# Four groups of TensorE matmuls in another order in each double step of a fused attention and convolution kernel

## The chip, the cores and the metric

The kernel runs on one core of a Trainium2 chip. The metric is the device time of one execution in microseconds (us), lower is better. The kernel before takes 6069.41 us, the median of three runs (6067.23 to 6069.91).

## The reference

The input x is 8 images of 192 channels, 128 by 128 pixels, all float32. Two layers follow one another. Layer 0 normalises x in 32 groups, projects every pixel to query, key and value (192 channels each, six heads of 32), and cuts each image into windows of 8 by 8 pixels, so 256 windows an image and 64 tokens a window. Per window and head:

```
o    = irfft2(rfft2(q * SCALE) * rfft2(k))          # 8 by 8 circular convolution, per channel
attn = softmax(o @ v^T + bias)                      # 64 x 64, bias depends on head and position
y    = attn @ v
x1   = x + proj(y) + proj_b
```

Layer 1 normalises x1 in 32 groups again, adds to every pixel its Laplacian (4 times itself less its four neighbours), multiplies by the 192 x 192 matrix merge_w, and adds merge_b and x1.

## The kernel before, in words

Everything is done in one long loop, software-pipelined by hand. The unit is a pair of windows side by side: 64 tokens each, so 128 tokens fill the partitions. There are 1024 pairs. A double step j handles two pairs and five stages of different age at once; `pair(lag)` in the code gives the double step that is in the stage of that lag, and is empty at the two ends of the loop. There are 512 double steps with attention work (j = 0 to 511), and then 76 in which only layer 1 is left.

In the double step j TensorE does in this order:

- `qkv(2j)`: query, key and value of the first new pair, ten matmuls into PSUM tile `b_q` (line 481).
- `m_slot(2j)`: a piece of layer 1's merge product, into `b_s` (lines 432 to 443), or nothing.
- half of the projection of lag 4 (lines 486 and 489).
- `qkv(2j+1)`, behind the semaphore `lo_out`: VectorE's remainder of the first pair (`qkl`, line 874) reads the same part of `b_q`.
- transposes of the values (line 518) and of lag 3's softmax P (line 528), the other half of the projection, `m_slot(2j+1)`.
- the group y = P times V of lag 3 (line 546), which waits for ScalarE's copy `probsT`; 48 matmuls in the trace.
- the inverse transform of lag 1 (line 556) from `prod` into `b_q`, 24 matmuls in the trace; it waits for `lo_out`.
- the forward transform of lag 0 (line 570) from `qkh` and `qkl` into the four banks of `b_t`, twelve matmuls; its second half waits for `yT_out`, since y lies in two of these banks.
- the scores of lag 1 (line 587) from `osb`, ScalarE's copy of the inverse transform, and `vT`, into `b_s`, 48 matmuls in the trace.

The scores write nearly all of `b_s`, which the merge pieces and the projection also use. So their first matmul waits for four semaphores: `o_out` (ScalarE has copied the inverse transform), `s_out`, `x1_done` (VectorE has taken the projection out, line 913) and `m_read` (VectorE has taken the merge piece of `m_slot(2j+1)` out, line 758).

VectorE goes through its own fixed list in each double step: the scores of lag 2 in its count, which are those that TensorE has just made, plus the bias (line 880), the maximum of them (L885), `qkl` of the first pair, the product of the two transforms (L891), statistics, the merge result (L758), one part of the stencil of layer 1 (lines 719, 727 and 735), `qkl` of the second pair, the sum of the softmax (L905), the projection's result (L913), the reciprocal (L923), in odd double steps the remainder `xhl` (L927), the merge result of `m_slot(2j+1)` (L758), and then border and statistics (L744, L621). GpSimd does two passes over the softmax (L1036 after the maximum, L1047 after the reciprocal) and in odd double steps the remainder `xl` (L1042), behind L1036. ScalarE copies out of PSUM (helper line 940) and does the exponential (L1004).

What a double step holds depends on j modulo 4; four double steps are one block of eight rows of pixels. In the texts below they are called a, b, c and d for j mod 4 = 0, 1, 2, 3. From block 18 on (of 0 to 127 with attention) the stencil runs, from block 19 on the merge pieces: two in each of a, b and c, none in d. The stencil's L735 stands in b, c and d; L927 and L1042 stand in b and d; the border L744 stands in d. In blocks in which the next image's statistics are gathered (the first 12 of 16 in an image) L621 stands at the end of each double step.

Of the kernel before, what the change touches and what calls it, by code (L numbers as in the profile page):

```python
# [16 lines left out]
N = WS * WS  # L17
QK, QKV = 2 * C, 3 * C
G, CG, GP = 32, 6, 4
EPS = 1e-5  # L20
NF = 94
# [72 lines left out]
def program(nc, x, out, w):  # L94
# [15 lines left out]
    with ExitStack() as ctx:  # L110
# [17 lines left out]
        fwd, fwdh, fwdl = sb("fwd_sb", [128, NF]), sb("fwdh", [128, NF], F32R), sb("fwdl", [128, NF], F32R)  # L128
        inv = sb("inv_sb", [NF, N])
# [227 lines left out]
        def _(pe):  # L357
            mm = nc.tensor.matmul
# [134 lines left out]
            for j, pair in doubles():  # L493
# [39 lines left out]
                if pair(4):  # L533
                    project(b_r[:, 256:512], 3).then_inc(proj_mm, 1)
                m_slot(2 * j + 1, pair)
                if pair(3):
                    k, n = pair(3)
                    pe.wait_ge(pT_out, n)
                    if pair(0):
                        pe.wait_ge(vT_out, pair(0)[1])  # L540
                    for i in range(2):
                        for h in range(NH):
                            for win in range(2):
                                rows = slice(win * N, (win + 1) * N)
                                q, c = (h * HD, i * N) if h < 4 else (i * N + (h - 4) * HD, 2 * N)
                                last = mm(q_banks[q:q + HD, 2 + win, c:c + N],  # L546
                                          vs[rows, (2 * k + i) % 8, h * HD:(h + 1) * HD],
                                          probsT[rows, i, h, :], start=True, stop=True)
                    last.then_inc(y_mm, 1)
                if pair(1):  # L550
                    pe.wait_ge(prod_done, pair(1)[1])
                    if pair(0):
                        pe.wait_ge(lo_out, 2 * j + 2)
                    for k in range(6):
                        for g in range(2):
                            last = mm(o_out_ps[g * N:(g + 1) * N, k * N:(k + 1) * N],  # L556
                                      prod[:, g * 6 + k, :, :].rearrange("p h d -> p (h d)"), inv[:, :],
                                      start=True, stop=True)
                    last.then_inc(o_mm, 1)
                if pair(0):  # L560
                    pe.wait_ge(lo_out, 2 * j + 2)
                    for i in range(2):
                        if i == 1 and pair(3):
                            pe.wait_ge(yT_out, pair(3)[1])
                        elif i == 1:
                            pe.wait_ge(vT_out, pair(0)[1])
                        for k, (ff, xx) in enumerate(((fwdh, qkh), (fwdh, qkl), (fwdl, qkh))):
                            for win in range(2):
                                rows = slice(win * N, (win + 1) * N)
                                last = mm(q_banks[0:NF, 2 * i + win, 0:QK], ff[rows, :], xx[rows, i, :],  # L570
                                          start=(k == 0), stop=(k == 2))
                    last.then_inc(t_mm, 1)
                if pair(1):
                    i, n = pair(1)
                    pe.wait_ge(o_out, n)
                    if pair(2):
                        pe.wait_ge(s_out, pair(2)[1])
                    if pair(4):
                        pe.wait_ge(x1_done, pair(4)[1])
                    pe.wait_ge(m_read, d_count[2 * j + 1])  # L580
                    for k in range(6):
                        for g in range(2):
                            for h in range(2):
                                s = g * 6 + k
                                t, q = divmod(s, 4)
                                r = (g * 2 + h) * HD
                                last = mm(scores[h * N:(h + 1) * N, s * N:(s + 1) * N], osb[r:r + HD, k, :],  # L587
                                          vT[r:r + HD, i % 2, q // 2, t - g, q % 2 * N:q % 2 * N + N],
                                          start=True, stop=True)
                    last.then_inc(s_mm, 1)  # L590

        @block.vector
        def _(dve):
# [341 lines left out]
        def _(act):  # L935
# [3 lines left out]
            def copy(o, i):  # L939
                return A.activation(o, i, ACT.Copy)  # L940
# [44 lines left out]
            for j, pair in doubles():  # L985
                blk, ph = divmod(2 * j, 8)
                img, c = divmod(blk, NS)
                if ph == 0 and c == 13 and 0 <= img < B - 1:
                    sqrt(cst[:, 3, :], cst[:, 2, :])
                if ph == 0 and c == 2 and 1 <= img <= B:  # L990
                    sqrt(sm[:, 6, :], sm[:, 4, :])
                h = (j + 2) // 2
                a_result(2 * j)
                if pair(0):
                    v_copy(2 * j)
                    high(2 * j)
                split(h, 0 if j % 2 == 0 else 2)
                if pair(0):
                    v_copy(2 * j + 1)
                if pair(2):  # L1000
                    i, n = pair(2)
                    act.wait_ge(sub_done, n)
                    pr = probs[:, i % 2, :, :].rearrange("p s m -> p (s m)")
                    A.activation(pr, pr, ACT.Exp).then_inc(exp_done, 1)  # L1004
                if pair(0):
                    high(2 * j + 1)
                    act.wait_ge(vT_mm, pair(0)[1])
                    copy(vT[:, j % 2, :, :, :].rearrange("p i t n -> p (i t n)"), q_banks[:, 2, :]).then_inc(vT_out, 1)
                if pair(3):
                    act.wait_ge(pT_mm, pair(3)[1])  # L1010
                    copy(probsT[:, :, :, :].rearrange("p i h n -> p i (h n)"), q_banks[:, 0:2, 0:6 * N]
                         ).then_inc(pT_out, 1)
                a_result(2 * j + 1)
                if j % 2 == 0:
                    split(h, 1)
                if pair(3):
                    act.wait_ge(y_mm, pair(3)[1])
                    copy(yT[:, :, :, :].rearrange("p i w n -> p w i n"),
                         q_banks[:, 2:4, 0:3 * N].rearrange("p w (i n) -> p w i n", n=N)).then_inc(yT_out, 1)
                if pair(1):  # L1020
                    act.wait_ge(o_mm, pair(1)[1])
                    copy(osb[:, :, :].rearrange("p k n -> p (k n)"), o_out_ps).then_inc(o_out, 1)
                if pair(0):
                    act.wait_ge(t_mm, pair(0)[1])
                    copy(qh[:, :, :], q_banks[0:NF, :, 0:C]).then_inc(qh_out, 1)
# [54 lines left out]
```

## Time and profile before

| quantity | value |
|---|---|
| median of 3 runs | 6069.41 us |
| the profiled execution | 6063.48 us |
| its span, first to last instruction | 6061.7 us |
| TensorE matmul busy | 5826.5 us, 96% |
| VectorE busy | 5059.8 us, 83% |
| ScalarE busy | 3165.5 us, 52% |
| GpSimd busy | 2011.1 us, 33% |
| granted TensorE clock, mean | 0.997 |

The profile is of one execution. Instruction starts are in us from the span's start. Matmuls overlap one another in the records, so the time of a group of matmuls is best read from its first start to the first start of the next group. TensorE's time between its groups is small; VectorE is the second busiest engine.

### The profile page before, as it was taken

The numbers are of one execution on the slowest core, as the hardware profiler recorded it, in microseconds if no ns is written. First come the engines' busy times: TensorE is split into PE (matmuls) and PEld (weight loads), VectorE is DVE, ScalarE is ACT, GpSimd is POOL, SyncE is SP. The second block draws the span as 40 slices with busy tenths as digits, with TensorE's granted clock in tenths as the row PEclk, the third lists the DMA queues.
The fourth block names the chain that finished last, engine by engine and source line by source line (L and its number), as shares of the span: only waits on it lengthen the run. The fifth ranks groups of instructions, "written<-read, shape, count | busy, mean of one in ns | idle before, by whom it ended". The sixth has DMA issues, their size and how long they took to land.

```text
span 6061.7 us, 210224 instructions
## 1 busy us (share of the span) xinstructions
PE 5826.5 (96%) x93708; PEld 5135.1 (85%) x93708; DVE 5059.8 (83%) x8287; ACT 3165.5 (52%) x6020; POOL 2011.1 (33%) x1286
## 2 busy tenths in 40 slices
PE   7999999999999999999999999999999999999987
PEld 5888888888888888888888888888888888888876
DVE  4777788888888888888888888888888888888876
ACT  2555555555555555555555555555555555555531
POOL 1333333333333333333333333333333333333310
PEclk9999999999999999999999999999999999999999
DMA  4221123323333233332333323332333322222235
GB/s 130 71 58 58 54 75 104 98 81 93 95 104 101 75 92 99 101 97 80 95 101 100 93 80 93 106 101 86 86 96 98 106 84 69 82 79 75 80 93 163
DMA packets 392599, 550.79 MB, mean 91 GB/s; under 512 B 24918, under 2 KB 284825, under 8 KB 391706
## 3 DMA queue, kind: packets, MB, share of 16 engines
q1 hardware_dynamic: 391708, 537.35, 30.9%
q8 instruction: 750, 12.29, 0.8%
q14 instruction: 141, 1.16, 0.1%
HBM read 335.93 MB, written 201.33 MB: 89 GB/s over the span
## 4 chain that ended last, share of the span: by engine, by line
PE 82%; DVE 8%; ACT 7%; issue 1%; DMA 1%; SPq 0%; DVEq 0%
PE b_q L481 22%; PE b_t L570 10%; PE b_s L587 7%; PE b_q L556 7%; PE b_t L546 6%; PE b_s L489 5%; PE b_s L486 5%; PE b_t L528 4%; PE b_s L432 3%; PE b_s L434 3%; PE b_t L518 3%; ACT qkh L940 2%; DVE qkl L874 2%; PE b_s L441 2%; PE b_s L443 2%; PE b_s L442 2%
## 5 line engine op out<-in xcount | busy, mean ns | idle before, releaser
L1047 POOL TENSOR_TENSOR probs<-probs,srec 128x768 f32<-128x768 f32 x512 | 880.7, 1720 | 2211.8 <-DVE srec L923 2211.8
L1036 POOL TENSOR_TENSOR probs<-probs,smax 128x768 f32<-128x768 f32 x512 | 754.1, 1473 | 1519.7 <-DVE smax L885 1519.7
L880 DVE TENSOR_TENSOR probs<-b_s,posb 128x768 f32<-128x768 f32 x512 | 488.3, 954 | 660.3 <-PE b_s L587 659.4
L940 ACT ACTIVATE vs<-b_q 128x192 f32<-128x192 f32 x1024 | 339.2, 331 | 1294.3 <-PE b_q L481 1294.3
L481 PE MATMUL b_q<-wnh,xh 128*128 128x288 f32 x2048 | 700.7, 342 | 67.0 <-DVE qkl L874 65.7
L874 DVE TENSOR_TENSOR qkl<-b_q,qkh 128x384 fp32r<-128x384 f32 x1024 | 566.5, 553 | 176.9 <-ACT qkh L940 139.7
L489 PEld LDWEIGHTS b_s<-yT,wp 128*128 128x128 f32 x4096 | 618.5, 191 | 52.3
L489 PE MATMUL b_s<-yT,wp 128*128 128x128 f32 x4096 | 622.4, 275 | 0.0
L486 PE MATMUL b_s<-yT,wp 128*128 128x256 f32 x2048 | 613.5, 381 | 1.5 <-DVE probs L880 0.9
L481 PE MATMUL b_q<-wnl,xhl 128*128 128x288 f32 x2048 | 606.5, 296 | 0.0
L481 PE MATMUL b_q<-wnh,xhb 128*128 128x288 f32 x2048 | 606.3, 296 | 0.0
L940 ACT ACTIVATE qh<-b_t 94x768 f32<-94x768 f32 x512 | 412.7, 806 | 369.7 <-PE b_t L570 369.7
L481 PE MATMUL b_q<-wnh,xl 128*128 128x288 f32 x2048 | 604.1, 295 | 0.0
L481 PE MATMUL b_q<-wnl,xh 128*128 128x288 f32 x2048 | 603.0, 294 | 0.0
L940 ACT ACTIVATE qkh<-b_q 128x384 fp32r<-128x384 f32 x1024 | 497.6, 486 | 166.4 <-PE b_q L481 166.4
L940 ACT ACTIVATE yT<-b_t 128x384 f32<-128x384 f32 x512 | 251.0, 490 | 629.3 <-PE b_t L546 629.3
L587 PEld LDWEIGHTS b_s<-vT,osb 32*64 32x64 f32 x24576 | 409.0, 133 | 174.7 <-issue 173.8
L587 PE MATMUL b_s<-vT,osb 32*64 32x64 f32 x24576 | 477.3, 221 | 27.1 <-DVE late L758 16.6
L885 DVE TENSOR_REDUCE smax<-probs 128x12 f32<-128x768 f32 x512 | 488.0, 953 | 17.7
L481 PEld LDWEIGHTS b_q<-wnh,xh 128*128 128x128 f32 x2048 | 387.2, 189 | 129.2 <-issue 94.7
L905 DVE TENSOR_REDUCE ssum<-probs 128x12 f32<-128x768 f32 x512 | 481.8, 941 | 0.0
L891 DVE TENSOR_TENSOR prod<-qh,b_t 94x768 f32<-94x768 f32 x512 | 481.2, 940 | 0.0
(155 smaller groups left out, 13688.6 us busy)
## 6 DMA issues: line engine op xcount, KB each, us to landing
ld<-in_x SPq DMA_DIRECT2D x192, 512.0 KB, 4.6
late<-x_dram SPq DMA_DIRECT2D x112, 640.0 KB, 4.8
xs<-in_x SPq DMA_DIRECT2D x128, 512.0 KB, 5.4
x_dram<-late SPq DMA_DIRECT2D x128, 512.0 KB, 3.0
out<-late SPq DMA_DIRECT2D x128, 512.0 KB, 3.0
late<-x_dram SPq DMA_DIRECT2D x240, 192.0 KB, 5.4
xs<-in_x SPq DMA_DIRECT2D x128, 256.0 KB, 5.9
x_dram<-late SPq DMA_DIRECT2D x128, 256.0 KB, 3.7
```

Of the source, the lines that this page charges most:

```text
L481: last = mm(o, xx[:, h % 2, at], ww[:, par, t, lo:up], start=(k == 0), stop=(k == 4))
L486: mm(o, wp[:, k, :], both, start=True, stop=False)
L489: last = mm(o.rearrange("p (r i w c) -> p i r w c", r=WS, i=2, w=2)[:, i], wp[:, k + 1 + i, :], rest, start=False, stop=(i == 1))
L570: last = mm(q_banks[0:NF, 2 * i + win, 0:QK], ff[rows, :], xx[rows, i, :], start=(k == 0), stop=(k == 2))
L587: last = mm(scores[h * N:(h + 1) * N, s * N:(s + 1) * N], osb[r:r + HD, k, :], vT[r:r + HD, i % 2, q // 2, t - g, q % 2 * N:q % 2 * N + N] ...
L874: V.tensor_tensor(qkl[:, i % 2, :], q_out, qkh[:, i % 2, :].bitcast(F32), ALU.subtract).then_inc(lo_out, 1)
L880: V.tensor_tensor(scored(i).rearrange("p (t q) m -> p t q m", q=4), scores.rearrange("p (t q m) -> p t q m", q=4, m=N), posb[:, :, :].unsq ...
L885: V.tensor_reduce(smax[:, i % 2, :], scored(i), AX.X, ALU.max).then_inc(max_done, 1)
L905: V.tensor_reduce(ssum[:, i % 2, :], scored(i), AX.X, ALU.add).then_inc(sum_done, 1)
L940: return A.activation(o, i, ACT.Copy)
L1036: P.tensor_tensor(probs[:, i % 2, :, :], probs[:, i % 2, :, :], smax[:, i % 2, :].unsqueeze(2).broadcast_to([128, 12, N]), ALU.subtract).t ...
L1047: P.tensor_tensor(probs[:, i % 2, :, :], probs[:, i % 2, :, :], srec[:, i % 2, :].unsqueeze(2).broadcast_to([128, 12, N]), ALU.mult).then_ ...
```

## The change

Line numbers in the diff's new part are those of the changed kernel. The double step's four last groups on TensorE stood in the order P times V, inverse transform, forward transform, scores. They now stand in the order inverse transform, P times V, scores, forward transform. Each keeps its own waits. On ScalarE the copy of the inverse transform (`osb`) now stands ahead of the copy of y (`yT`). VectorE's, GpSimd's and the DMA queue's lists are not touched, and no instruction is added or removed.

```
@@ TensorE, double step j, behind m_slot(2 * j + 1, pair) @@
+                if pair(1):
+                    pe.wait_ge(prod_done, pair(1)[1])
+                    if pair(0):
+                        pe.wait_ge(lo_out, 2 * j + 2)
+                    for k in range(6):
+                        for g in range(2):
+                            last = mm(o_out_ps[g * N:(g + 1) * N, k * N:(k + 1) * N],
+                                      prod[:, g * 6 + k, :, :].rearrange("p h d -> p (h d)"), inv[:, :],
+                                      start=True, stop=True)
+                    last.then_inc(o_mm, 1)
                 if pair(3):
                     k, n = pair(3)
                     pe.wait_ge(pT_out, n)
...
                     last.then_inc(y_mm, 1)
-                if pair(1):
-                    pe.wait_ge(prod_done, pair(1)[1])
...
-                    last.then_inc(o_mm, 1)
-                if pair(0):
-                    pe.wait_ge(lo_out, 2 * j + 2)
-                    for i in range(2):
-                        if i == 1 and pair(3):
-                            pe.wait_ge(yT_out, pair(3)[1])
-                        elif i == 1:
-                            pe.wait_ge(vT_out, pair(0)[1])
...
-                    last.then_inc(t_mm, 1)
                 if pair(1):
                     i, n = pair(1)
                     pe.wait_ge(o_out, n)
                     if pair(2):
                         pe.wait_ge(s_out, pair(2)[1])
                     if pair(4):
                         pe.wait_ge(x1_done, pair(4)[1])
                     pe.wait_ge(m_read, d_count[2 * j + 1])
...
                     last.then_inc(s_mm, 1)
+                if pair(0):
+                    pe.wait_ge(lo_out, 2 * j + 2)
+                    for i in range(2):
+                        if i == 1 and pair(3):
+                            pe.wait_ge(yT_out, pair(3)[1])
+                        elif i == 1:
+                            pe.wait_ge(vT_out, pair(0)[1])
+                        for k, (ff, xx) in enumerate(((fwdh, qkh), (fwdh, qkl), (fwdl, qkh))):
+                            for win in range(2):
+                                rows = slice(win * N, (win + 1) * N)
+                                last = mm(q_banks[0:NF, 2 * i + win, 0:QK], ff[rows, :], xx[rows, i, :],
+                                          start=(k == 0), stop=(k == 2))
+                    last.then_inc(t_mm, 1)
@@ ScalarE, double step j, last three copies @@
+                if pair(1):
+                    act.wait_ge(o_mm, pair(1)[1])
+                    copy(osb[:, :, :].rearrange("p k n -> p (k n)"), o_out_ps).then_inc(o_out, 1)
                 if pair(3):
                     act.wait_ge(y_mm, pair(3)[1])
                     copy(yT[:, :, :, :].rearrange("p i w n -> p w i n"),
                          q_banks[:, 2:4, 0:3 * N].rearrange("p w (i n) -> p w i n", n=N)).then_inc(yT_out, 1)
-                if pair(1):
-                    act.wait_ge(o_mm, pair(1)[1])
-                    copy(osb[:, :, :].rearrange("p k n -> p (k n)"), o_out_ps).then_inc(o_out, 1)
```

On TensorE, from the second m_slot of a steady double step to the next double step's qkv, the program before has these rows, with what each first matmul waits for (L546 is P times V, L556 the inverse transform, L570 the forward transform, L587 the scores):

```order
L434 MATMUL b_s<-late,mn 128x256
L546 MATMUL b_t<-probsT,vs 32x64 [waits vT_out,pT_out]
L546 MATMUL b_t<-probsT,vs 32x64 x23
L556 MATMUL b_q<-inv_sb,prod 64x64 [waits lo_out,prod_done]
L556 MATMUL b_q<-inv_sb,prod 64x64 x11
L570 MATMUL b_t<-qkh,fwdh 94x384 [waits lo_out]
L570 MATMUL b_t<-qkh,fwdh 94x384 [waits yT_out]
L587 MATMUL b_s<-vT,osb 64x64 [waits x1_done,m_read,s_out,o_out]
L587 MATMUL b_s<-vT,osb 64x64 x23
L481 MATMUL b_q<-wnh,xh 128x288 [waits xhl_done,xl_done,xh_done]
```

The changed program has these there, at the same place (its L542 is the inverse transform, L556 P times V, L574 the scores, L588 the forward transform):

```order
L434 MATMUL b_s<-late,mn 128x256
L542 MATMUL b_q<-inv_sb,prod 64x64 [waits lo_out,prod_done]
L542 MATMUL b_q<-inv_sb,prod 64x64 x11
L556 MATMUL b_t<-probsT,vs 32x64 [waits vT_out,pT_out]
L556 MATMUL b_t<-probsT,vs 32x64 x23
L574 MATMUL b_s<-vT,osb 64x64 [waits x1_done,m_read,s_out,o_out]
L574 MATMUL b_s<-vT,osb 64x64 x23
L588 MATMUL b_t<-qkh,fwdh 94x384 [waits lo_out]
L588 MATMUL b_t<-qkh,fwdh 94x384 [waits yT_out]
L481 MATMUL b_q<-wnh,xh 128x288 [waits xhl_done,xl_done,xh_done]
```

The scores, with their four semaphores, moved from behind the forward transform to ahead of it; the inverse transform is now the first of the four.

On ScalarE, the copies at the end of a double step and the first of the next, before:

```order
L940 ACTIVATE probsT<-b_t 128x768 [waits pT_mm]
L940 ACTIVATE yT<-b_t 128x2x3x64 [waits y_mm]
L940 ACTIVATE osb<-b_q 128x384 [waits o_mm]
L940 ACTIVATE qh<-b_t 94x768 [waits t_mm]
L940 ACTIVATE vs<-b_q 128x192 [waits v_mm]
```

and in the changed program:

```order
L940 ACTIVATE probsT<-b_t 128x768 [waits pT_mm]
L940 ACTIVATE osb<-b_q 128x384 [waits o_mm]
L940 ACTIVATE yT<-b_t 128x2x3x64 [waits y_mm]
L940 ACTIVATE qh<-b_t 94x768 [waits t_mm]
L940 ACTIVATE vs<-b_q 128x192 [waits v_mm]
```

The copies yT and osb have changed places; qh, the copy of the forward transform, still follows them.

## Rows read from the trace of the kernel before

**Rows 1.** Page, part 4: the chain that ended last, by engine.

```profile
PE 82%; DVE 8%; ACT 7%; issue 1%; DMA 1%; SPq 0%; DVEq 0%
```

**Rows 2.** Waits of TensorE: total us, times, longest us.

```profile
PE b_q L481 <- DVE qkl L874: 65.7, 164, 1.3
PE b_s L587 <- DVE late L758: 16.6, 12, 1.5
PE b_s L432 <- issue: 15.9, 60, 1.1
```

**Rows 3.** Timeline, TensorE, a step b: start us, us, instruction [idle before <-releaser].

```profile
3433.16 0.40 PE L481 MATMUL b_q<-wnh,xh 128*128 128x288 f32 x1
...
3440.63 0.77 PE L546 MATMUL b_t<-probsT,vs 64*32 64x64 f32 x48
...
3442.18 0.41 PE L570 MATMUL b_t<-qkh,fwdh 64*94 64x384 f32 x2
...
3443.56 0.93 PE L587 MATMUL b_s<-vT,osb 32*64 32x64 f32 x48
```

**Rows 4.** Timeline, VectorE, the same step b.

```profile
3435.31 0.56 DVE L874 TENSOR_TENSOR qkl<-b_q,qkh 128x384 fp32r<-128x384 f32 x1
...
3437.64 0.96 DVE L735 SCALAR_TENSOR_TENSOR late<-late 128x512 f32<-128x512 f32 x1
...
3442.93 0.48 DVE L758 SCALAR_TENSOR_TENSOR late<-b_s,mc,late 128x256 f32<-128x256 f32 x1
...
3444.54 0.96 DVE L880 TENSOR_TENSOR probs<-b_s,posb 128x768 f32<-128x768 f32 x1 [0.53 <-PE b_s L587]
```

**Rows 5.** Timeline, ScalarE, the start of the same step b.

```profile
3434.13 0.33 ACT L940 ACTIVATE vs<-b_q 128x192 f32<-128x192 f32 x1 [0.90 <-PE b_q L481]
3434.79 0.49 ACT L940 ACTIVATE qkh<-b_q 128x384 fp32r<-128x384 f32 x1 [0.33 <-PE b_q L481]
```

**Rows 6.** Timeline, GpSimd, xl in the step b and in the next step d.

```profile
3436.76 1.29 POOL L1042 TENSOR_TENSOR xl<-xs,xh 128x512 fp32r<-128x512 f32 x1
...
3459.96 1.74 POOL L1042 TENSOR_TENSOR xl<-xs,xh 128x512 fp32r<-128x512 f32 x1
```

**Rows 7.** Timeline, VectorE, L735 in the step c between.

```profile
3448.89 0.68 DVE L735 SCALAR_TENSOR_TENSOR late<-late 128x512 f32<-128x512 f32 x1
```

**Rows 8.** Timeline, VectorE, ScalarE and TensorE, that step d.

```profile
3460.46 1.78 DVE L735 SCALAR_TENSOR_TENSOR late<-late 128x512 f32<-128x512 f32 x1
...
3461.12 0.48 ACT L940 ACTIVATE qkh<-b_q 128x384 fp32r<-128x384 f32 x1
...
3461.97 0.82 ACT L940 ACTIVATE probsT<-b_t 128x768 f32<-128x768 f32 x1
...
3462.17 0.54 DVE L874 TENSOR_TENSOR qkl<-b_q,qkh 128x384 fp32r<-128x384 f32 x1
3462.19 0.61 PE L489 MATMUL b_s<-yT,wp 128*128 128x128 f32 x4
...
3462.84 0.77 PE L546 MATMUL b_t<-probsT,vs 64*32 64x64 f32 x48
...
3465.60 0.93 PE L587 MATMUL b_s<-vT,osb 32*64 32x64 f32 x48
```

**Rows 9.** Timeline, TensorE, the start of the step a behind it; and a step b.

```profile
3466.46 0.40 PE L481 MATMUL b_q<-wnh,xh 128*128 128x288 f32 x1
...
3469.99 0.38 PE L481 MATMUL b_q<-wnh,xh 128*128 128x288 f32 x1
...
3436.25 0.38 PE L481 MATMUL b_q<-wnh,xh 128*128 128x288 f32 x1
```

**Rows 10.** Timeline, the one double step without forward transform, j = 512.

```profile
5833.68 0.92 PE L556 MATMUL b_q<-inv_sb,prod 94*64 94x64 f32 x24
...
5834.65 0.49 ACT L940 ACTIVATE osb<-b_q 128x384 f32<-128x384 f32 x1 [0.37 <-PE b_q L556]
5835.19 0.93 PE L587 MATMUL b_s<-vT,osb 32*64 32x64 f32 x48 [0.59 <-ACT osb L940]
```

More of the change, by code:

```diff
@@ L549, in _ @@
                     last.then_inc(y_mm, 1)
-                if pair(1):
-                    pe.wait_ge(prod_done, pair(1)[1])
-                    if pair(0):
-                        pe.wait_ge(lo_out, 2 * j + 2)
[L554 to L558, printed above, removed]
-                    last.then_inc(o_mm, 1)
-                if pair(0):
-                    pe.wait_ge(lo_out, 2 * j + 2)
-                    for i in range(2):
-                        if i == 1 and pair(3):
-                            pe.wait_ge(yT_out, pair(3)[1])
-                        elif i == 1:
-                            pe.wait_ge(vT_out, pair(0)[1])
[L567 to L571, printed above, removed]
-                    last.then_inc(t_mm, 1)
                 if pair(1):
```

## The prediction

> **What bounds the kernel now.** I read the chain of waits first. It lies on TensorE for 82% of the span, with 8% on VectorE and 7% on ScalarE [rows 1]. So the order of matmuls costs nothing by itself: the same groups run one after another, and the time changes only where a wait appears or goes. The list of TensorE's waits gives the named ones: 65.7 us in front of `qkv(2j+1)` for `qkl`, 16.6 us in front of the scores for VectorE's merge result, and 60 waits of 15.9 us in front of a merge piece [rows 2]. Then I read the timelines of all engines through one block of four double steps, because the pattern repeats block by block, and asked for each group that moves: what releases it, and how long before it starts.
>
> **Lengths of the groups.** A group's last matmul is modelled to end 0.07 us behind the first start of the next group where nothing waits: the scores of step d end at 3465.60 + 0.93 = 3466.53, and `qkv` starts at 3466.46 [rows 8, 9]. First start to first start, P times V and inverse transform together take 3442.18 - 3440.63 = 1.55 us in step b [rows 3], of which 0.77 - 0.07 = 0.70 is P times V and 0.85 the inverse transform. The scores take 3466.46 - 3465.60 = 0.86. In step d, P times V, inverse and forward transform take 3465.60 - 3462.84 = 2.76 together [rows 8], so the forward transform takes 2.76 - 1.55 = 1.21. In step b 1.38 passes between its start and the scores', so a wait lies in that.
>
> **Part 1, the scores come 1.21 us earlier behind their semaphores.** This is the costly part. In step b VectorE has the longest list: it ends the merge result at 3442.93 + 0.48 = 3443.41, and the scores start at 3443.56, 0.15 later [rows 3, 4]. In the old order the forward transform fills the time: without any wait the scores would start at 3442.18 + 1.21 = 3443.39, so 0.17 us is lost. In the new order the two groups ahead of the scores end at 3440.63 + 0.85 + 0.70 = 3442.18; the scores stand until 3443.56, which is 1.38 us, and the forward transform comes afterwards in full. Behind the waiting matmul is all of TensorE, and VectorE's L880 waits for it too. The loss is 1.38 - 0.17 = 1.21 us, if VectorE ends at the same time.
>
> Can VectorE be earlier? It receives the scores 1.21 us earlier, counted from the next `qkv`, so L880 and L885 move up. But L874 stands behind ScalarE's copy: qkh ends at 3434.79 + 0.49 = 3435.28 and L874 starts at 3435.31, with no idle time noted in front of it [rows 4, 5]. That copy hangs on `qkv(2j)`, which is not moved. So VectorE's list behind L874 keeps its place. One instruction in it gets shorter: L735 takes 0.68 in step c [rows 7], 0.96 in step b [rows 4] and 1.78 in step d [rows 8]. In b and d its end is 0.5 us behind the end of GpSimd's L1042: 3438.05 and 3438.60, 3461.70 and 3462.24 [rows 4, 6, 8]. L1042 follows the pass after the maximum, so it moves up by up to 1.21 us: it would end at 3436.84 in b and, with 1.29 us, at 3460.04 in d, ahead of L735's starts at 3437.64 and 3460.46. L735 is then 0.68 in both. In b that takes 0.28 us off the loss: 1.21 - 0.28 = 0.93. The piece in b stands in blocks 19 to 127, 109 of them: **+101 us** (without the relief 109 x 1.21 = 132; with VectorE also earlier through L874, 0).
>
> The Trainium skill, "SBUF — State Buffer", section "SBUF: two separate sides", says that VectorE instructions with two SBUF inputs and GpSimd instructions lock a shared port pair against one another, so that the loser blocks for the whole instruction. The trace agrees: L735 reads two SBUF tensors and ends only behind L1042. By the lock the sum is the one with the relief, and if these were only slow instructions it would be 31 us more.
>
> **Part 2, waits that go.** In step d there is no merge piece. P times V starts at 3462.84, when probsT (3461.97 + 0.82 = 3462.79) is there; the projection ahead of it ends at 3462.19 + 0.61 = 3462.80, so 3462.73 would have been possible and 0.11 us is lost [rows 8]. The inverse transform now stands there and waits instead for L874, which ends at 3462.71; at 0.15 behind that it would start at 3462.86, no gain [rows 8]. But with L735 1.10 us shorter, L874 is bounded only by qkh, 3461.60, and comes 0.56 earlier. Then nothing waits: 109 x 0.11 = **-12 us**; and in the first 18 blocks, whose 72 double steps have the probsT wait and no stencil, 72 x 0.11 = **-8 us**. Between -20 and 0.
>
> **Part 3, step a.** `qkv(2j+1)` starts 3469.99 - 3466.46 = 3.53 us behind `qkv(2j)` in the step a shown, and 3436.25 - 3433.16 = 3.09 in a step b with the same list [rows 3, 9]. The 0.44 us is the merge piece waiting for L880, which VectorE begins late because step d's list was long. It occurs in the 60 waits of [rows 2]. With step d's list 0.56 us shorter it goes: up to 60 x 0.44 = 26 us. I take **-19**, as the chain from L735 through the border to L880 has to stay free; bounds -26 and 0.
>
> **Part 4, the irregular double steps** (image changes, where VectorE's chains of small instructions run): VectorE ends last there, with waits of up to 1.5 us in front of the scores already now, 12 of them [rows 2]. Each loses the cover of 1.21 us: 12 x 1.21 = 15, and some more that were just covered. I take **+20**, bounds 0 and 40.
>
> **Part 5, edits at nothing.** ScalarE's osb is now covered by P times V alone. The double step j = 512 has no forward transform and shows the shortest way: inverse transform from 5833.68, osb, scores at 5835.19, which is 1.51 us [rows 10]; the new order has 0.85 + 0.70 = 1.55. It is hidden by 0.04 us; if the wait took VectorE's 0.15 us behind osb, 1.61 would come out, 0.06 x some 400 = 24 us. The copy qh moves 0.85 us towards v_copy, in front of which ScalarE idles 0.90 [rows 5]: hidden by 0.05; without that cover each 0.1 us costs 50 us over 512 steps. yT has the whole score group before the forward transform's second half needs it. No DMA moves.
>
> **Sum.** 101 - 12 - 8 - 19 + 20 = +82. On the profiled execution 6063.5 + 82 = 6145.5; the median of the runs is 5.9 above it, so 6069.4 + 82 = 6151 us.
>
> **Rivals.**
> - *VectorE follows the scores.* If L885's end, and not qkh, sets L874, VectorE's list moves up with the scores. Then step b loses nothing and the 65.7 us of waits for `qkl` go too: 6069 - 66 - 19 - 20 = 5964. For it: no idle time is noted in front of L874, so L885 ends close to it. Against it: L874 starts 0.03 us behind qkh's end [rows 4, 5], and the qkh copy depends on `qkv(2j)`, which no longer follows the scores. It decides if L874 can start well ahead of 2.1 us behind `qkv(2j)`. Chance 0.07.
> - *No relief from GpSimd.* L735 stays long: 132 in part 1, 0 in part 3, part 2 only the -8, 20 in part 4: +144, 6213. For it: the relief in d rests on L1042 being 0.4 us clear. Chance 0.12.
> - *A narrow cover fails in every step* (osb or qh, part 5): +24 to +50 on top, around 6190. For it: covers of 0.04 and 0.05. Chance 0.15.
> - *Gains and losses meet*: only half of part 1 comes, as VectorE finds slack elsewhere, with parts 2 and 3 in full, and no part 4: +50 - 46 = 6073. Chance 0.05.
> - The forecast itself: 0.61.
>
> The sum's own bounds are 101 to 132, -20 to 0, -26 to 0, 0 to 40. 6098 to 6205 holds the forecast, the third rival and part of the second. What a measurement can tell from no change is about 0.2%, 12 us: faster 0.08, within 0.03, slower 0.89.
>
> **What the profile of the changed kernel would show.** Idle time in front of the scores released by VectorE's L758, about 1.1 us, once in four double steps, some 110 us in all; L735 at 0.68 in every block; step d's L874 behind qkh at once; the 60 waits in front of a merge piece gone; osb and qh waiting as long as now for TensorE, and no wait of the scores for osb. L880 in step b starting before `qkv` does. I am wrong if L758 of step b ends 1.2 us earlier counted from `qkv(2j)`, or if the scores wait for osb in all steps.

## The result and the profile after

Measured: **6236.56 us** (median of 4 runs, 6235.06 to 6238.25) against 6068.32 (4 runs of the kernel before on the same chip, 6065.76 to 6069.91). The ratio is 1.0277 with a 95% interval from 1.0265 to 1.0289: 168 us slower, twice the +82 that was forecast, and outside the stated range of 6098 to 6205.

In the new code the groups have the lines L542 (inverse transform), L556 (P times V), L574 (scores) and L588 (forward transform); VectorE's and ScalarE's lines kept their numbers. The page of the changed kernel, its parts 1 and 4, and one row of part 3:

```profile
span 6236.5 us, 210224 instructions
PE 5854.7 (94%) x93708; PEld 5165.7 (83%) x93708; DVE 4918.0 (79%) x8287; ACT 3168.8 (51%) x6020; POOL 1952.9 (31%) x1286
q8 instruction: 750, 12.29, 0.8%
PE 71%; DVE 21%; ACT 4%; issue 2%; DMA 0%; SPq 0%; DVEq 0%
```

TensorE's share of the chain fell from 82% [rows 1] to 71%, and VectorE's rose from 8% to 21%: an engine that had been busy all through now waits. TensorE's waits (total us, times, longest us) name four places that answer to [rows 2]:

```profile
PE b_s L574 <- DVE late L758: 146.7, 140, 2.0
PE b_q L481 <- DVE qkl L874: 73.4, 176, 1.3
PE b_s L574 <- issue: 40.0, 51, 1.7
PE b_s L432 <- issue: 1.7, 4, 0.4
```

The first row is the predicted wait; before it had 16.6 us in 12 places. The last is the merge piece, 15.9 us in 60 places before. The third was in no step of the prediction. It releases nothing: "issue" is time in which TensorE waited for nothing that the profile shows.

A step b of the changed kernel, all engines. The columns are start us, duration us, instruction, and the idle time before it with its releaser; the rows answer to [rows 3 to 6]:

```profile
3537.27 0.49 ACT L940 ACTIVATE qkh<-b_q 128x384 fp32r<-128x384 f32 x1 [0.33 <-PE b_q L481]
3537.79 0.56 DVE L874 TENSOR_TENSOR qkl<-b_q,qkh 128x384 fp32r<-128x384 f32 x1 [1.30 <-ACT qkh L940]
3538.01 1.27 POOL L1042 TENSOR_TENSOR xl<-xs,xh 128x512 fp32r<-128x512 f32 x1
...
3540.12 0.68 DVE L735 SCALAR_TENSOR_TENSOR late<-late 128x512 f32<-128x512 f32 x1
...
3543.11 0.92 PE L542 MATMUL b_q<-inv_sb,prod 94*64 94x64 f32 x24
...
3543.95 0.77 PE L556 MATMUL b_t<-probsT,vs 64*32 64x64 f32 x48
...
3545.13 0.48 DVE L758 SCALAR_TENSOR_TENSOR late<-b_s,mc,late 128x256 f32<-128x256 f32 x1
...
3545.76 0.93 PE L574 MATMUL b_s<-vT,osb 32*64 32x64 f32 x48 [1.03 <-DVE late L758]
3546.61 0.41 PE L588 MATMUL b_t<-qkh,fwdh 64*94 64x384 f32 x2
3546.74 0.96 DVE L880 TENSOR_TENSOR probs<-b_s,posb 128x768 f32<-128x768 f32 x1 [0.53 <-PE b_s L574]
```

This is the step as the prediction had it. VectorE now stands idle for 1.30 us in front of L874, which still starts 0.03 us behind qkh's end. L758 ends at 3545.61 and the scores start 0.15 us later. From the start of P times V to the scores it is 1.81 us where 0.70 would do: 1.11 lost, less the 0.17 of before, 0.94. GpSimd's xl ends at 3539.28, ahead of L735, which takes 0.68 us.

**Where the 175 us between the two profiled executions are.** I cut both traces at the first `qkv` of each of the first 512 double steps, which gives 511 stretches, and subtracted step from step. They hold 176 us; ahead of them and behind them the changed kernel is 1.3 us shorter. A step has a "gap" when two matmuls that follow one another inside one group start more than 0.6 us apart. "Regular" are steps without gap and half clock whose difference is under 0.5 us or, in a step b with a merge piece (blocks 19 to 127), between 0.8 and 1.05 us.

| steps | number | after minus before, us |
|---|---|---|
| regular b, blocks 19 to 127 | 92 | +85.8 |
| regular a, c, d | 100, 115, 98 | -16.0, +0.2, -2.1 |
| regular b, blocks before 19 | 13 | -0.8 |
| steps with a gap inside the scores or the forward transform | 47 | +49.7 |
| steps that a half-clock stretch touches | 26 | +42.1 |
| other irregular steps | 20 | +17.1 |
| sum | 511 | +176.0 |

So the predicted waits came as computed, and the steps with gaps and with half clock cost about half of the total. Of the steps that half clock touches 12 are steps b; about 11 of their 42 us are the ordinary 0.93 of such a step.

**The gaps.** TensorE alone, in a step where nothing was awaited:

```profile
4046.47 0.77 PE L556 MATMUL b_t<-probsT,vs 64*32 64x64 f32 x48
4047.17 0.69 PE L574 MATMUL b_s<-vT,osb 32*64 32x64 f32 x32
4048.75 0.46 PE L574 MATMUL b_s<-vT,osb 32*64 32x64 f32 x16 [0.89 <-issue]
4049.14 0.41 PE L588 MATMUL b_t<-qkh,fwdh 64*94 64x384 f32 x2
```

The scores begin on time, stop after 32 of 48 matmuls, and go on 0.89 us later. No instruction between them waits on a semaphore. Counting TensorE's instructions from the program's start and from 0 (each matmul, each weight load and each semaphore instruction one), the first one behind the gap is at place 193 modulo 256 in all 51 gaps; from the start before to the start behind they last 1.06 us on average, 53.9 us together. Queue q8, "instruction" in the page, moves 750 packets of 16,384 bytes in both kernels. The packet that belongs to this gap started at 4046.23 and landed at 4047.33, 1.42 us before the scores went on; over the 51 gaps that is 1.2 to 1.6 us. The kernel before has one such gap, of 0.67 us. My reading: TensorE ran out of instructions. Two more readings of the traces speak for it. TensorE's 192,069 instructions fill 750 packets of 256. And with a packet to each boundary, the instruction at place 193 never starts sooner than 1.07 us behind the landing of its packet (1.23 in the kernel before), while the median distance is 4.7 us (5.3). The packets ahead of the gaps were not slow (1.10 us against 1.07 for the others) but began late, 3.9 us on average behind the boundary before against 2.2; why they did stays open. Most boundaries cost nothing: of 191 that fall into the scores 46 bring a gap, of the 290 in the inverse transform and P times V none.

**The half clock.** Busy time of each engine in two stretches, then TensorE's granted clock (PEclk), the DMA share and GB/s; and the groups in the second stretch:

```profile
3500.00:3506.00 6.00, 6.00 (x73) 5.42 (x64) 4.14 (x6) 2.14 (x4) 1.68 (x2) 1.00 0.75 183
3822.50:3828.00 5.50, 5.01 (x117) 4.05 (x113) 4.30 (x8) 0.98 (x2) 1.47 (x1) 0.50 0.43 146
```

```profile
3820.51 0.70 PE L432 MATMUL b_s<-late,mn 128*128 128x256 f32 x2 [1.84 <-DVE late L758]
...
3824.50 1.56 PE L574 MATMUL b_s<-vT,osb 32*64 32x64 f32 x48 [0.49 <-DVE late L758]
3825.99 0.63 PE L588 MATMUL b_t<-qkh,fwdh 64*94 64x384 f32 x2
3826.42 0.52 PE L588 MATMUL b_t<-qkl,fwdh 64*94 64x384 f32 x2
3826.74 0.52 PE L588 MATMUL b_t<-qkh,fwdl 64*94 64x384 f32 x2
3827.06 0.52 PE L588 MATMUL b_t<-qkh,fwdh 64*94 64x384 f32 x2
```

The granted clock is 0.50 here, the lower of TensorE's two levels (1.2 instead of 2.4 GHz). The scores take 1.49 us to the next group instead of 0.86, and a pair of the forward transform 0.32 instead of 0.17. Before it the engine had stood 1.84 us for L758 in an image change. Until 6000 us the changed kernel has 15 such stretches of 3.4 to 6.8 us, 71.7 us together; the kernel before has two in its attention part, 6.8 us together. Each of them begins behind a stop of 1 us or more, or inside one. But such a stop alone does not bring the clock down: this wait of 1.84 us stands in the same six double steps of both kernels, and half clock follows in four of them after the change and in one before.

### The profile page after: what moved, and what is told of

Same layout as the page of the kernel before. It is cut to its first block, busy times and chain, and to the rows that moved or that the text cites. A ratio compares the mean times of both kernels' runs of the same rounds, so it can differ in the third digit from the quotient of the medians.

```text
span 6236.5 us, 210224 instructions
## 1 busy us (share of the span) xinstructions
PE 5854.7 (94%) x93708; PEld 5165.7 (83%) x93708; DVE 4918.0 (79%) x8287; ACT 3168.8 (51%) x6020; POOL 1952.9 (31%) x1286
## 4 chain that ended last, share of the span: by engine, by line
PE 71%; DVE 21%; ACT 4%; issue 2%; DMA 0%; SPq 0%; DVEq 0%
PE b_q L481 21%; PE b_t L588 10%; PE b_s L574 7%; PE b_q L542 5%; PE b_s L489 4%; PE b_s L486 4%; PE b_t L556 4%; DVE qkl L874 4%; PE b_t L528 4%; PE b_t L518 3%; ACT qkh L940 2%; DVE ssum L905 2%; DVE late L758 2%; DVE late L913 2%; DVE prod L891 2%
## 5 line engine op out<-in xcount | busy, mean ns | idle before, releaser
L1047 POOL TENSOR_TENSOR probs<-probs,srec 128x768 f32<-128x768 f32 x512 | 880.2, 1719 | 2744.7 <-DVE srec L923 2744.7
L874 DVE TENSOR_TENSOR qkl<-b_q,qkh 128x384 fp32r<-128x384 f32 x1024 | 568.7, 555 | 790.4 <-ACT qkh L940 785.8
L574 PE MATMUL b_s<-vT,osb 32*64 32x64 f32 x24576 | 498.3, 223 | 193.9 <-DVE late L758 146.7
L574 PEld LDWEIGHTS b_s<-vT,osb 32*64 32x64 f32 x24576 | 424.0, 134 | 252.3 <-issue 194.2
L940 ACT ACTIVATE osb<-b_q 128x384 f32<-128x384 f32 x512 | 251.8, 492 | 687.5 <-PE b_q L542 687.5
L542 PEld LDWEIGHTS b_q<-inv_sb,prod 94*64 94x64 f32 x12288 | 401.8, 138 | 144.1 <-issue 125.1
```

Source lines behind the costliest of these rows:

```text
L542: last = mm(o_out_ps[g * N:(g + 1) * N, k * N:(k + 1) * N], prod[:, g * 6 + k, :, :].rearrange("p h d -> p (h d)"), inv[:, :], start=True, ...
L874: V.tensor_tensor(qkl[:, i % 2, :], q_out, qkh[:, i % 2, :].bitcast(F32), ALU.subtract).then_inc(lo_out, 1)
L1047: P.tensor_tensor(probs[:, i % 2, :, :], probs[:, i % 2, :, :], srec[:, i % 2, :].unsqueeze(2).broadcast_to([128, 12, N]), ALU.mult).then_ ...
```

## The experiments

The theory after the result, called A: the order lost (1) the cover of the scores in step b, some 100 us, (2) the time between groups that issue 48, 96 and 96 instructions in 0.85, 0.70 and 0.86 us, so that TensorE outruns its instruction packets, some 50 us, and (3) some 60 us where it stands longer in image changes and the clock falls. The rivals stand with each run.

### e1_o_first: inverse transform first, scores last

Only the first half of the change: inverse transform, P times V, forward transform, scores. The diffs of e1 and of e3 to e7 are against the changed kernel, those of e10 to e12 against the kernel before.

```diff
                     last.then_inc(y_mm, 1)
+                if pair(0):
+                    pe.wait_ge(lo_out, 2 * j + 2)
...
+                    last.then_inc(t_mm, 1)
                 if pair(1):
...
                     last.then_inc(s_mm, 1)
-                if pair(0):
-                    pe.wait_ge(lo_out, 2 * j + 2)
...
-                    last.then_inc(t_mm, 1)
```

> Order: inverse transform, P times V, forward transform, scores (the scores stay last); osb ahead of yT on ScalarE. This is the half of the change that moves only the inverse transform. Theory A (the changed kernel lost about 120 us because the scores wait uncovered for VectorE, and some 60 to 80 us because TensorE runs out of instructions inside the scores where P times V and scores follow one another directly): none of the two losses comes, only the probsT wait of part 2 goes in the early blocks: 6052 to 6069 us, at most 2 starvation gaps inside the scores. Rival B (putting the inverse transform first costs by itself, through lo_out or through osb): 6080 us or more.

Measured: 6127.34 (6120.07 to 6130.44), ratio 1.0098 (1.0083 to 1.0113). 109 us less than the full change, but 61 above before, so the time that A gave it was missed. It lies in the range of rival B, though neither `lo_out` nor osb is the cause. The trace shows what is:

```profile
3442.39 0.41 PE L570 MATMUL b_t<-qkh,fwdh 64*94 64x384 f32 x2
3442.50 0.49 ACT L940 ACTIVATE yT<-b_t 128x384 f32<-128x384 f32 x1 [0.20 <-PE b_t L556]
3442.64 0.34 PE L570 MATMUL b_t<-qkl,fwdh 64*94 64x384 f32 x2
3442.82 0.34 PE L570 MATMUL b_t<-qkh,fwdl 64*94 64x384 f32 x2
3443.04 0.41 PE L570 MATMUL b_t<-qkh,fwdh 64*94 64x384 f32 x2
```

The second half of the forward transform starts 0.05 us behind ScalarE's yT, 0.22 after the pair before it instead of 0.17, and its first pair is slower again (0.25 to the next). yT frees the bank that it writes, and now only the first half of the forward transform lies between. The whole group takes 1.34 us instead of 1.21 in all steps but b, where the wait for L758 hides it: about 50 us over some 400 steps. In the first 19 blocks and in step a it is nearly paid back, by probsT's wait of 0.12 us and by part of the merge piece's wait, so that c and d are 0.12 and 0.14 us longer (medians) and a and b 0.02. By the table's measure the regular steps cost +35 us, the 11 steps with gaps +13, the others +11. Cover is lost in a place that the full change does not touch, since there the scores stand ahead of the forward transform.

### e3_half_t: half of the forward transform ahead of the scores

```diff
                     last.then_inc(y_mm, 1)
+                if pair(0):
+                    pe.wait_ge(lo_out, 2 * j + 2)
...
+                            mm(q_banks[0:NF, win, 0:QK], ff[rows, :], xx[rows, 0, :],
+                               start=(k == 0), stop=(k == 2))
                 if pair(1):
```

> Changed kernel, but the first half of the forward transform (six matmuls into the first two banks, 0.6 us) stands between P times V and the scores, the second half behind the scores. Same matmuls, same number of instructions. Theory A: the wait for VectorE in step b falls from 1.10 to 0.50 us, 109 times, so 65 us less, and the gaps inside the scores mostly go, another 50 to 60 us: about 6110 to 6125 us. Rival C (no instruction starvation; the 1 us gaps inside the scores are something that the scores bring wherever they wait): only the 65 us, about 6170 us, and some 50 gaps remain.

Measured: 6195.47 (6184.08 to 6196.28), ratio 1.0208 (1.0193 to 1.0223). Both expectations missed, A's by 70 us. Step b did fall from +0.93 to +0.41 us (median), and the gaps from 51 to 21, as half a cover should do. But steps a and c, which wait for nothing there, became 0.16 and 0.17 us longer. Each half of the forward transform takes 0.70 us to the next group where the whole took 1.22, so two more starts of a group cost 0.18 us a step, some 0.09 each, which eats the rest of the gain. The tile shape changes at each (64*94, then 32*64, then 64*94), but that it is the shape is not shown: in e1 the second half of the forward transform, behind a short wait and in one shape, loses the same 0.08. The waits:

```profile
PE b_s L581 <- DVE late L763: 51.0, 119, 1.3
PE b_s L581 <- issue: 20.0, 33, 1.8
```

### e4_merge_first: VectorE's merge result ahead of xhl

The changed kernel, with VectorE ending the merge result (L758) before it makes xhl in odd double steps, 0.69 us earlier.

```diff
                     V.reciprocal(srec[:, i % 2, :], ssum[:, i % 2, :]).then_inc(rec_done, 1)
+                m_result(2 * j + 1)
                 h = (j + 2) // 2
...
-                m_result(2 * j + 1)
                 borders(2 * j + 1)
```

> Changed kernel, but in odd double steps VectorE takes out the merge result of the second m_slot (line 758) ahead of the remainder xhl (line 927), so it is ready 0.7 us earlier. TensorE's list is the changed kernel's. Theory A: the wait in front of the scores in step b falls from 1.10 to about 0.4 us, 109 times: 75 us less, about 6160 us, and the gaps inside the scores stay at about 50, because TensorE's instructions come as before. Rival D (VectorE's total load, not the place of line 758, sets the wait): no change, 6230 us or more.

Measured: 6142.23 (6133.34 to 6152.55), ratio 1.0126 (1.0109 to 1.0143), 94 us less than the full change, where A had 75. The waits, to be held against those of the kernel after:

```profile
PE b_q L481 <- DVE qkl L874: 72.6, 176, 1.3
PE b_s L574 <- issue: 40.9, 59, 1.5
...
PE b_s L574 <- DVE late L758: 35.8, 40, 1.1
```

Taking one instruction from in front of L758 takes 111 us from its wait, and step b falls from +0.93 to +0.04. That shows the size of part 1 by its removal. The issue row does not move (40.0 and 40.9), and 45 of its 50 gaps lie in double steps that have one in the changed kernel too: the gaps are no consequence of the wait. What is left above the kernel before, +74 us over the steps, is mainly gaps, 47 steps and +51, half-clock stretches, 14 steps and +18 (26 and +42 in the full change), and step a with -17 in its regular and +17 in its irregular steps. The edit has a price of its own, seen in e12: xhl now takes 1.13 us on average instead of 0.69.

### e5_space_y_s and e6_space_o_y: a spacer in the burst

One matmul of 128x128 by 128x512 in float32 is added in each double step: 4 instructions. In e5 it stands between P times V and the scores, in e6 between the inverse transform and P times V. It writes a bank whose content the forward transform overwrites afterwards; the lines are the same in both.

```diff
+                if pair(3) and pair(0):
+                    pe.wait_ge(pT_out, pair(3)[1])
+                    mm(q_banks[:, 0, :], ident[:, :], wq[:, 0, 0:512], start=True, stop=True)
```

> Changed kernel with one more matmul (128x128 by 512 columns, float32, four instructions, about 0.86 us, its result is thrown away) between P times V and the scores in each double step that has both. It gives TensorE time without instructions at this place. It costs 0.86 us in some 400 steps and nothing in step b, where it lies in the wait for VectorE: +330 to +350 us. Theory A (instruction starvation inside the scores): the gaps of about 1 us inside the scores go nearly all, -55 us: about 6510 us. Rival C: the gaps stay, about 6570 us.

> The same extra matmul, but between the inverse transform and P times V, so that P times V and scores still follow one another directly. Same work, same number of instructions and same slack for VectorE as in the kernel with the spacer between P times V and scores. Theory A: the gaps inside the scores stay in part (20 or more), so it is slower than the other spacer kernel by 20 to 55 us. Rival C: the two take the same time within 10 us.

Measured: e5 6554.05 (6553.17 to 6557.16), ratio 1.0799 (1.0782 to 1.0815); e6 6556.46 (6553.41 to 6561.75), ratio 1.0802 (1.0786 to 1.0819). The spacer costs 1.05 us a step (median of step c), not the 0.86 I had set, which is why A's number for e5 was too low. In-group gaps fall to 3 in e5 and 7 in e6, and TensorE's wait for L758 to 10.7 and 10.5 us. So A's statement that e6 would keep its gaps is wrong, and the two take the same time, as rival C had it, though the gaps that C wanted to stay are gone: it is not the meeting of P times V and the scores that starves TensorE, but the three dense groups together, 240 instructions in 2.41 us, and a pause anywhere in them is enough. That the gaps go with added time speaks for a supply and against a fixed cost of the instruction at that place.

### e7_pad: the same program, shifted by 128 instructions

```diff
             pe.wait_ge(pos_done, 1)
+            for _ in range(32):
+                mm(m_out[:, 0:1], ident[:, :], pb[:, 0:1], start=True, stop=True)
```

> Changed kernel with 32 tiny float32 matmuls (128 TensorE instructions, some 2 us) ahead of the loop. Everything in the loop is the same, but each boundary of 256 instructions in TensorE's stream lies 128 instructions elsewhere. Theory A (TensorE's gaps of about 1 us inside the scores are a wait for the next 256 instructions): about as many gaps (35 to 65), about the same time (6230 to 6250 us), and every gap again just where the count of instructions crosses the same place modulo 256, so inside other double steps or at other places of the group than in the changed kernel. Rival C (the gaps come from data or semaphores): the gaps stand in the same double steps as in the changed kernel.

Measured: 6255.13, one run without an interval. That is 5 us above A's range; the loop begins 14.6 us later, and the 511 stretches hold 177 us more than in the kernel before, as against 176 in the changed kernel. It has 48 gaps, all of them again at place 193 modulo 256, though every step's instructions now have other numbers. Only one of the 48 double steps with a gap is among the 51 that have one in the changed kernel. That is the clearest separation of the study: the gaps belong to the boundary of the instruction packets and not to image changes, data or a double step.

### e10_xl_first: the kernel before, with GpSimd's xl ahead

The relief of L735 needs no new order of TensorE: it comes when GpSimd makes xl before the pass after the maximum.

```diff
             for j, pair in doubles():
+                h = (j + 2) // 2
+                if j % 2 == 1 and 0 <= h < PAIRS // 4:
+                    pool.wait_ge(xh_done, 3 * h + 2)
+                    P.tensor_tensor(tokens(xl, 0, h), windows(0, h), tokens(xh, 0, h).bitcast(F32), ALU.subtract
+                                    ).then_inc(xl_done, 1)
                 if pair(2):
```

> Kernel before, but GpSimd does xl (line 1042) ahead of the pass after the maximum (line 1036) instead of behind it in odd double steps. Theory A: VectorE's L735 is held only by GpSimd's L1042 and takes 0.68 us in b, c and d; the wait of the scores in step b (0.17 us, 109 times) goes and the merge piece in step a waits no longer (up to 26 us): 6025 to 6045 us. Rival E (lateness of the softmax pass or of xl takes its place): 6065 us or more.

Measured: **6033.58** (6029.10 to 6039.03), against 6068.31, ratio 0.9943 (0.9930 to 0.9955). Faster than both kernels, and inside A's range. L735 in the kernels before, after and e10 (times it runs, busy us, mean ns), from the lines grouped by instruction:

```profile
L735 DVE SCALAR_TENSOR_TENSOR late<-late 128x512 f32<-128x512 f32 x384 | 398.3, 1037 | 0.7
```

```profile
L735 DVE SCALAR_TENSOR_TENSOR late<-late 128x512 f32<-128x512 f32 x384 | 261.7, 682 | 0.7
```

```profile
L735 DVE SCALAR_TENSOR_TENSOR late<-late 128x512 f32<-128x512 f32 x384 | 259.6, 676 | 0.7
```

and what is left of TensorE's waits at the merge piece and at the scores in e10:

```profile
PE b_s L432 <- issue: 2.6, 6, 1.1
PE b_s L587 <- DVE late L758: 7.0, 12, 0.8
```

Step a is 0.42 us shorter and step b 0.16 (medians): the merge piece's wait of 0.44, and the 0.17 in front of the scores, both of which the prediction read off the kernel before. It has 3 gaps.

### e9, e11, e12: the merge result first in the other orders

The edit of e4 on top of e1 (e9), on top of e10 (e11), and on the kernel before alone (e12).

> Kernel before with the inverse transform first, scores last, and the merge result ahead of xhl on VectorE in odd double steps. If the 0.17 us that the scores wait for line 758 in step b of the kernel before is what remains there, it goes: 109 x 0.17 = 18 us less than with the inverse transform first alone, about 6040 to 6050 us. If something else stands behind it at once (the remainder xhl late for the next qkv, or line 880), 6055 us or more.

> As the kernel before with xl first on GpSimd, and on VectorE the merge result of the second m_slot ahead of xhl in odd double steps. Nothing should be left for it to gain in regular steps; in irregular ones up to 10 us: the same time as with xl first alone, or up to 10 us less.

> Kernel before with the merge result ahead of xhl on VectorE in odd double steps, nothing else. The 0.17 us wait of the scores in step b goes, 18 us; if line 880 of step c then starts late by as much, because VectorE's list is as long as before, half or all of it is lost again: 6050 to 6069 us.

Measured: e9 6136.56 (6131.33 to 6143.39), ratio 1.0110 (1.0093 to 1.0127): nothing gained over e1, where 18 us were expected, and 87 us above the first range given. e11 6040.18 (6036.96 to 6040.65), 0.9951 (0.9939 to 0.9964): no better than e10. e12 6085.38 (6083.99 to 6089.76), 1.0030 (1.0019 to 1.0041): slower than before and 16 us above its range. Step b's wait of 0.17 us at the scores does go in e12, but 0.18 us in front of the next `qkv` takes its place: xhl has become the late one. A row grows that is 1.3 us, once, in the kernel before:

```profile
PE b_q L481 <- DVE xhl L928: 11.3, 13, 1.3
```

and step c, where neither kernel waited, is 0.22 us longer. xhl starts only 0.34 us later in step b, but ends 1.39 us later (medians), since it takes 1.74 us there instead of 0.69. In the kernel before it starts 0.05 us ahead of GpSimd's pass L1047, in e12 0.28 us behind it, and then it ends only 0.5 us behind that pass. Its rows in the kernel before and in e12:

```profile
L927 DVE TENSOR_TENSOR xhl<-xs,xhl 64x512 fp32r<-64x512 f32 x256 | 175.5, 685 | 8.1
```

```profile
L928 DVE TENSOR_TENSOR xhl<-xs,xhl 64x512 fp32r<-64x512 f32 x256 | 290.2, 1133 | 8.0
```

It is the same meeting as that of L735 with xl, and e4, e9 and e11 have it too (1.13 us on average in each).

## Why the prediction was wrong, by its own steps

- **What bounds the kernel.** "So the order of matmuls costs nothing by itself: the same groups run one after another, and the time changes only where a wait appears or goes." This is the step that failed. The term missing in the sum is the instruction supply: about +50 us, shown by the 51 gaps at one place of 256, by e7 (the gaps move with the count), by e5 and e6 (time inside the burst takes them away) and by e4 (they stay when the wait goes). The forward transform was not only cover for VectorE, it was also 1.21 us with 24 instructions between the 144 of P times V and inverse transform and the 96 of the scores. Rows for it were there: 48, 96 and 96 instructions by 0.85, 0.70 and 0.86 us give 10 ns an instruction on average, against 50 ns in the forward transform. The 50 counts gaps over 0.6 us; with all stops over 0.15 us at that place, close behind a landing, it is 76 and 64 us, where the kernel before has 7 and 2 us.
- **Part 1**, +101. Mechanism and size were right: +0.93 us in the median step b, as computed, and +86 us over the 92 steps that are regular; +110 over all steps b, with their irregular ones. L874 stayed behind qkh: its wait for ScalarE rose from 139.7 us in 186 places to 785.8 in 745, VectorE being early and held there. L735's relief is exact (398.3 to 261.7 us). The rivals "VectorE follows the scores" and "no relief from GpSimd" are refuted by that.
- **Part 2**, -20. Over-sized. The probsT wait went in the steps named; step d is 0.1 us shorter in 60 of them. But the regular steps d give only -2.1 us, since 19 of them are 0.2 to 0.5 us longer, and those of the first 19 blocks -3.1 us where -8 was set. Short stops at place 193 lie in some of these steps; the others are not explained.
- **Part 3**, -19. -16 in the regular steps a; the row of the merge piece fell from 15.9 to 1.7 us.
- **Part 4**, +20. Mis-sized: the irregular steps cost +17 and those with half clock +42, so 59, of which some 12 are the ordinary loss of 13 steps b. The 15 us of lost cover assumed that TensorE keeps its speed through a longer wait. It didn't: the longest waits of the scores grew from 1.5 to 2.0 us, the granted clock fell to 0.50 behind 15 stops, and the groups that followed took 1.7 to 1.9 times as long. e4 shows the link in part: with the wait shortened there are 8 stretches in place of 15, and their steps cost +18 in place of +42.
- **Part 5**, nothing. Right for osb (1.2 us of waits in all), qh and yT in this order. e1 shows how thin such a cover is: with the forward transform straight behind P times V, yT costs 0.13 us in every step that does not wait there anyway, about 50 us.
- **Sum.** The four parts measured are about 86 - 19 + 59 = +126, and with the 50 of the gaps +176. The forecast's 82 lacks the 50 and 39 of part 4; the rest is 5. Added up, the sum's own upper bounds (132, 0, 0 and 40) allow +172, which is 6241 us and would hold the measured time, but for reasons that did not occur: L735 was relieved, and no bound had the gaps in it. The stated range was narrower than its terms.

How much the half clock costs by itself is open: no run here kept the longer waits and the clock. That each half-clock stretch follows a long wait is seen in the traces, not shown by an edit. The four runs of e4 point the same way: the longest (6152.6 us) has the lowest mean granted clock (0.992) and the shortest (6133.3) the highest (0.995).

The Trainium skill, "Runtime: NRT & Kernel Launch", section "Instruction fetch mechanics", says that an engine's instructions arrive in 16 KiB blocks of 256, fetched through a DMA queue of the sequencer, and that this is "mostly hidden". The trace agrees on the block (16,384 bytes, gaps at one place of 256 instructions) and not on the hiding: at 10 ns an instruction about a quarter of the boundaries that fall into the scores cost about 1 us each.

## What to carry to other kernels

Before reordering an engine that is never idle, write beside each group not only its time but its instructions and who must be finished at its start: a long group of few instructions covers other engines' lists and the supply of instructions alike. If the gain sought lies in another engine's release (here GpSimd's xl, which slowed L735), move that instruction and leave the tight engine alone: e10 took 35 us off where the new order added 168. Whatever is moved on VectorE, look at what GpSimd runs at the new place: moving xhl by a third of a microsecond made it take 1.74 us instead of 0.69. And price a wait on TensorE in an already irregular stretch at more than its length, since the clock may fall behind it.

## What the runs showed of the hardware

- TensorE can stand 1.06 us (mean of 51, start to start) at one place of every 256 instructions when small matmuls with a weight load each run at about 10 ns an instruction for 2.41 us; 46 of the 191 boundaries in the scores do it. It goes on 1.2 to 1.6 us behind the landing of a packet of 16,384 bytes. One pause of about a microsecond in such a burst cuts the gaps from 51 to 3 or 7.
- Two more starts of a group cost 0.18 us a step in e3 (0.70 + 0.70 in place of 1.22); the spacer of e5 costs 1.05 us a step where 0.86 was expected. Whether tile shape, wait or pipeline makes it, no run tells.
- Half clock lasts 3.4 to 6.8 us a time in the attention part and lengthens the scores from 0.86 to 1.49 us and a forward pair from 0.17 to 0.32. All half-clock time, the program's end included, is 33.3 us before and 105.3 after.
- L735 takes 0.68 us alone and up to 1.78 while GpSimd works on its xl; e10 shows it by moving GpSimd's instruction alone. xhl takes 0.69 us when it starts ahead of GpSimd's L1047 and 1.74 us when it starts behind it (e12, step b).
